# Depthwise filters as Toeplitz products per channel, and chunk products with the four heads on four tiles of the array

## What is computed

```python
def _L1_attn_ref(hidden_states, ...):                # H, DK, DV, CHUNK = 4, 32, 32, 32
    q, k, v_direct = conv(h @ Wq), conv(h @ Wk), conv(h @ Wv)     # 4 taps, silu
    beta = sigmoid(h @ Wb)
    delta_out = _delta_rule_chunkwise(q, k, v_direct, beta)
    paths = [_fir(v_direct, f) for f in (fir_w3, fir_w7, fir_w15, fir_w31)] + [delta_out]
    hmid = gelu(concat([h] + paths) @ router_W1 + router_b1)
    probs = softmax((hmid @ router_W2 + router_b2) / tau)
    ctx = sum(probs[..., i:i+1] * paths[i] for i in range(5))
    ...                                                # gate with v_direct, norm, Wo

def _fir(x, filt):            # causal depthwise filter: each channel has its own taps
    y[t, c] = sum over j < K of filt[c, j] * x[t - (K - 1) + j, c]     # K = 3, 7, 15, 31

def _delta_rule_chunkwise(q, k, v, beta, chunk=32):
    A = kb @ kc.T per chunk;  T = I + tril(A, -1);  inv = T^-1
    u = inv @ vc;  w = inv @ kbc
    for each of the 4 chunks:                          # S is the state, 32 x 32 per head
        u_adj = u_i - w_i @ S
        o = q_i @ S + tril(q_i @ k_i.T) @ u_adj
        S = S + k_i.T @ u_adj
```

## Time and profile before

| | |
|---|---|
| median of 3 runs | 1063.66 us |
| all three | 1063.66, 1056.33, 2446.21 us |
| span of the profiled execution | 1056.7 us |
| PE, DVE, ACT, POOL busy | 986.0, 735.5, 667.3, 331.7 us |
| instructions | 21902 |

### The profile page before, as it was taken

One profiled execution on the slowest core, in us unless ns is written; L12 is line 12 of the kernel. 1 busy time (PEld: TensorE's weight loads), 2 busy tenths in 40 slices (PEclk: granted clock), 3 DMA queues, 4 the chain that ended last, 5 costly groups with the idle time before them and its releaser, 6 DMA issues.

```text
span 1056.7 us, 21902 instructions
## 1 busy us (share of the span) xinstructions
PE 986.0 (93%) x7958; PEld 642.1 (61%) x7958; DVE 735.5 (70%) x2802; ACT 667.3 (63%) x1508; POOL 331.7 (31%) x720
## 2 busy tenths in 40 slices
PE   7989899999997989999999999999978999999996
PEld 4777475544446566568776756654436675677675
DVE  2656779788978766557544688887887786857523
ACT  4499998875532224676988777847533335677753
POOL 3775342524022011435332422241320022423321
PEclk9999999999986879999999999999986999999999
DMA  9300001031441110010000000204442010000001
GB/s 320 139 2 1 1 1 51 2 80 44 89 86 37 19 36 27 11 41 21 2 11 1 11 1 21 50 12 96 95 91 43 11 32 11 11 11 2 11 1 30
DMA packets 71930, 41.23 MB, mean 39 GB/s; under 512 B 52368, under 2 KB 64144, under 8 KB 71568
## 3 DMA queue, kind: packets, MB, share of 16 engines
q1 hardware_dynamic: 71824, 39.84, 14.6%
HBM read 30.92 MB, written 8.91 MB: 38 GB/s over the span
## 4 chain that ended last, share of the span: by engine, by line
PE 48%; DVE 27%; ACT 15%; POOL 4%; issue 3%; DMA 2%; SPq 1%; POOLq 0%; ACTq 0%; DVEq 0%
PE psum L1060 6%; DVE pool L1541 5%; DVE sol_t L1546 4%; PE psum L953 4%; ACT pool L1770 4%; PE psum L521 4%; DVE pool L1490 3%; PE psum L1050 3%; PE psum L883 3%; PE psum L796 2%; PE psum L794 2%; PE psum L822 2%; PE psum L1046 2%; PE psum L1044 2%; PE psum L922 2%
## 5 line engine op out<-in xcount | busy, mean ns | idle before, releaser
L1756 ACT ACTIVATE pool<-psum 128x512 f32<-128x512 f32 x144 | 84.2, 600 | 87.9 <-PE psum L883 38.9
L1770 ACT ACTIVATE pool<-pool,small 128x128 f32<-128x128 f32 x224 | 91.7, 487 | 37.6 <-POOL small L2135 37.5
L521 PE MATMUL psum<-sb_const,pool 128*128 128x128 f32 x672 | 100.0, 283 | 12.2 <-ACT pool L1770 8.1
L2130 POOL TENSOR_SCALAR small<-small 128x4 f32<-128x4 f32 x88 | 22.4, 254 | 272.2 <-DVE small L1132 270.7
L521 PEld LDWEIGHTS psum<-sb_const,pool 128*128 128x128 f32 x672 | 78.2, 144 | 47.7 <-issue 23.4
L883 PE MATMUL psum<-pool,firw 128*32 128x512 f32 (+7 forms) x960 | 105.4, 581 | 0.0
L2133 POOL TENSOR_TENSOR small<-small,minus_half 128x4 f32<-128x4 f32 x88 | 93.3, 1061 | 7.3
L953 PE MATMUL psum<-pool,sb_l1a 128*128 128x512 f32 x192 | 92.3, 634 | 0.7 <-ACT pool L1756 0.7
L1060 PEld LDWEIGHTS psum<-sb_l1f,pool 128*128 128x128 f32 x640 | 78.2, 192 | 14.5 <-issue 12.6
L1060 PE MATMUL psum<-sb_l1f,pool 128*128 128x128 f32 x640 | 83.3, 278 | 0.0
L1363 DVE TENSOR_TENSOR pool<-pool,psum 128x512 f32<-128x512 f32 x80 | 52.6, 680 | 31.3 <-ACT pool L1895 12.9
(11 more groups left out here) (427 smaller groups left out, 2248.2 us busy)
## 6 DMA issues: line engine op xcount, KB each, us to landing
pool<-scratch_kk SPq DMA_DIRECT2D x18, 256.0 KB, 3.7
pool<-in_cF SPq DMA_DIRECT2D x16, 256.0 KB, 3.5
pool<-in_xF SPq DMA_DIRECT2D x8, 256.0 KB, 6.0
pool<-in_x SPq DMA_DIRECT2D x8, 256.0 KB, 6.2
scratch_xt<-pool SPq DMA_DIRECT2D x8, 256.0 KB, 2.0
pool<-scratch_xt SPq DMA_DIRECT2D x8, 256.0 KB, 3.1
scratch_kk<-pool SPq DMA_DIRECT2D x32, 64.0 KB, 1.9
scratch_xt<-pool SPq DMA_DIRECT2D x16, 128.0 KB, 2.6
```

Of the source, the lines that this page charges most:

```text
L521: m = e.transpose(f.ap[:, part(b)], src[:, part(b)], ident)
L1756: e.activation(slot(g, i), f.ap, ACT.Copy).then_inc(f.emptied, 1)
L1770: m = e.activation(dst[:, part(b)], src[:, part(b)], ACT.Identity, bias=v["nm"][:, b:b + 1], scale=v["r"][:, b:b + 1])
```

## The change

**Filters.** v of the group (time-major, slot 2) goes to a padded DRAM array with 32 zero rows ahead of each entry. Four DMAs read it back in windows: partition i of quarter r holds row 16 n + i of the channels 32 r to 32 r + 31, for each block n of 16 time steps. Two more DMAs inside SBUF cut this into "this window" and "the window one block earlier". A table `toeplitz` [128, 32, 80] holds for every channel the taps of the four filters as 16-column Toeplitz blocks (64 columns), and another 16 columns for the part of the longest filter that reaches into the earlier window. b_fir.k now means channel quarter k, not filter length: for every channel one matmul of 32 rows, 32 weights (the windows of that channel, read at a stride of 32 elements) and 64 columns of the table, and one of 16 columns for the longest filter. The result has (block, channel) on the wrong axes for the rest of the kernel, so it goes to DRAM in pieces of 16 elements (b_fs) and is read back by channel (b_fl). b_r and b_mx wait for that.

**Chunk products.** b_u and b_p keep their 16 products a step, but head h now lies on rows and columns 32h to 32h + 31 (b_p: columns), so neighbours in the order use different tiles. For that the right side and the inverses are laid out by head: new DMA steps b_rs and b_rl (right side out and back), and b_xt apart from b_xo. b_p's subtraction is 128x128 instead of 32x512. b_u's copy is four pieces of 32x128: two by DVE, two by ACT, the second of which waits for DVE.

**The rest.** A set-up, lay_windows, builds the table with 97 DMAs in two rounds behind the weight loads. GpSimd zeroes the table at the start; b_ez is gone. Three constants that are used once move to a slot of group 0. ORDER is a new table (1839 entries instead of 1775).

```diff
+TB, NBLK, NROW = 16, P // 16, P // 16 + 2
+NVF = 5
...
-    firw, itau = sb("firw", [P, nfg * 4, CH]), sb("inverse_tau", [P, NH])
+    toeplitz, itau = sb("toeplitz", [P, CH, NVF * TB]), sb("inverse_tau", [P, NH])
+    lags = nc.dram_tensor("scratch_taps", (P, NVF * TB), F32, kind="Internal").ap()
+    padded = nc.dram_tensor("scratch_v", (NB, P + CH, P), F32, kind="Internal").ap()
+    paths = nc.dram_tensor("scratch_fir", (NG, 4, CH, P, TB), F32, kind="Internal").ap()
...
         def b_sh(g, k):
-            o.wait_ge(sem("v_made"), g + 1)
+            f = fill("b_vT", g)
+            o.wait_ge(f.emptied, f.n)
             upper_half(o, g)
-            e.dma_start(kept, slot(g, 5)).then_inc(sem(f"v_out{a}"), 16)
-            o.wait_ge(sem(f"v_out{a}"), 16 * (g // NA + 1))
-            for s in range(4):
-                e.dma_start(vsh[32 * s:32 * s + 32, :, s:],
-                            kept.rearrange("(c p) m -> p c m", c=4)[:, :, 0:GT - s]).then_inc(sem(f"shifted{a}"), 16)
+            e.dma_start(padded[g * GB:g * GB + GB, CH:, :].rearrange("b t c -> t b c"), b4(slot(g, 2))).then_inc(*path(g))
+            moved(o, g, "v")
+            for r in range(4):
+                src = bass.AP(padded.tensor, padded[g * GB].offset + CH * r, [[P, CH], [TB * P, GB * NROW - 1], [1, CH]])
+                e.dma_start(windows(g)[CH * r:CH * r + CH, 0:GB * NROW - 1], src).then_inc(*path(g))
+
+        def b_sw(g, k):
+            moved(o, g, "rows")
+            for early in range(2):
+                src = windows(g).rearrange("p (b n) c -> p b (n c)", b=GB)[:, :, CH * (1 - early):CH * (NBLK + 1 - early)]
+                e.dma_start(slot(g, 8 + 2 * early, 2).rearrange("p (b m) -> p b m", b=GB), src).then_inc(*path(g))
+
+        def b_fs(g, k):
+            f = fill("b_fir", g, "s", k)
+            o.wait_ge(f.emptied, f.n)
+            dst = paths[g, k].rearrange("n p t -> p n t")
+            e.dma_start(dst, slot(g, 3 + k).rearrange("p (n t) -> p n t", t=TB)).then_inc(*path(g))
+
+        def b_fl(g, k):
+            moved(o, g, "sums")
+            by_channel = paths[g].rearrange("r (u f) (j n) t -> j (r u) f (n t)", f=4, j=4)
+            for j in range(4):
+                e.dma_start(slot(g, 3, 4)[j:P:4].rearrange("p (f m) -> p f m", f=4), by_channel[j]).then_inc(*path(g))
...
         def b_fir(g, k):
-            vsh = slot(g, 8, 4).rearrange("p (c b t) -> p c b t", c=4, b=GB)
-            kgs = [kg for ff, kg in FIR_GROUPS if ff == k]
-            for n, kg in enumerate(kgs):
-                for c in range(4):
-                    col = FIR_GROUPS.index((k, kg)) * 4 + c
-                    m = e.matmul(b4(f.ap)[32 * c:32 * c + 32, :, 4 * kg:], firw[:, col, :],
-                                 vsh[:, c, :, 0:P - 4 * kg], start=n == 0, stop=n == len(kgs) - 1)
+            o.wait_ge(sem("toeplitz_laid"), 32 + 16 * 16 * len(FIRS) + 16 * (CH - 1))
+            moved(o, g, "windows")
+            shifted = [slot(g, 8 + 2 * early, 2).rearrange("p (n c) -> p n c", c=CH) for early in range(2)]
+            f, r_ = begin("b_fir", g, "s", k), slice(CH * k, CH * k + CH)
+            for u in range(8):
+                for early in (0, 1):
+                    for j in range(4):
+                        c, j_ = 4 * u + j, slice(32 * j, 32 * j + 32)
+                        lo, hi = (48, 64) if early else (0, 64)
+                        m = e.matmul(f.ap[j_, 64 * u + lo:64 * u + hi], shifted[early][r_, :, c],
+                                     toeplitz[r_, c, 64 * early:64 * early + hi - lo], start=not early, stop=bool(early))
             m.then_inc(f.filled, 1)
...
         def b_p(g, k):                                 # PE
-            for q in range(NP):
-                m = e.matmul(hd(f.ap)[CH * c:CH * c + CH, q, :], kkt[0:CH * c, q, CH * c:CH * c + CH],
-                             hd(slot(g, 14))[0:CH * c, q, :], start=True, stop=True)
+            for b in range(GB):
+                for h in range(NH):
+                    q = h * GB + b
+                    m = e.matmul(f.ap[CH * h:CH * h + CH, DH * b:DH * b + DH], kkt[0:CH * c, q, CH * c:CH * c + CH],
+                                 hd(slot(g, 14))[0:CH * c, q, :], start=True, stop=True)
...
         def b_u(g, k):                                 # PE
-            src = hd(slot(g, 12 if c else 14))
-            for q in range(NP):
-                m = e.matmul(hd(f.ap)[r_, q, :], hd(slot(g, 13))[r_, q, :], src[r_, q, :], start=True, stop=True)
+            for b in range(GB):
+                for h in range(NH):
+                    h_, n = slice(CH * h, CH * h + CH), b * 4 + c
+                    m = e.matmul(f.ap[h_, DH * b:DH * b + DH], hd(slot(g, 13))[h_, n, :], hd(slot(g, 12))[h_, c * GB + b, :],
+                                 start=True, stop=True)
...
         def b_r(g, k):
-            got("b_fir", g, "s", 3)
+            moved(o, g, "paths")
...
         def b_p(g, k):                                 # DVE
-            e.tensor_tensor(slot(g, 12)[r_], slot(g, 14)[r_], f.ap[r_], ALU.subtract).then_inc(f.emptied, 1)
+            f, rest = full("b_p", g, "s", k), slot(g, 12)[:, P * (k + 1):P * (k + 2)]
+            e.tensor_tensor(rest, rest, f.ap[:, 0:P], ALU.subtract).then_inc(f.emptied, 1)
+
+        def b_u(g, k):                                 # DVE
+            f, r_ = full("b_u", g, "s", k), slice(CH * k, CH * k + CH)
+            for h in range(NH // 2, NH):
+                m = e.tensor_copy(slot(g, 14)[r_, part(h)], f.ap[CH * h:CH * h + CH, 0:P])
+            m.then_inc(sem("u_halves"), 1)
...
         def b_u(g, k):                                 # ACT
-            e.activation(slot(g, 14)[r_], f.ap[r_], ACT.Copy).then_inc(f.emptied, 1)
+            e.activation(slot(g, 14)[r_, part(0)], f.ap[0:CH, 0:P], ACT.Copy)
+            o.wait_ge(sem("u_halves"), n_half["b_u", k, g])
+            e.activation(slot(g, 14)[r_, part(1)], f.ap[CH:2 * CH, 0:P], ACT.Copy).then_inc(f.emptied, 1)
```

More of the change, by code:

```diff
@@ L1 @@
+import itertools
 from contextlib import ExitStack
@@ L313, in wt @@
         n = width - lo if n is None else n
+        if piece in once_used:
+            return spare[piece][:, lo:lo + n]
+        first -= sum(cols[p_][apart][1] for apart, of in once_used.items() if of == p_ and cols[p_][apart][0] < first)
         return tiles[p_][:, first + lo:first + lo + n]
@@ L363, in landed, with windows, path, moved @@
         for p_ in parts:
-            own.wait_ge(sem("ld_" + p_), 16)
+            own.wait_ge(sem("ld_" + p_), 16 * landing.get(p_, 1))
+    def windows(g):
+        return slot(g, 3, 3)[:, 0:GB * NROW * CH].rearrange("p (n c) -> p n c", c=CH)
+    MOVED = {"v": 1, "rows": 5, "windows": 7, "sums": 11, "paths": 15}
+    def path(g):
+        return sem(f"path{g % NA}"), 16
+    def moved(own, g, what):
+        own.wait_ge(sem(f"path{g % NA}"), 16 * (g // NA * MOVED["paths"] + MOVED[what]))
+    CHUNKED = {"diagonals": 4, "triangles": 6, "inverses": 8, "turned": 12}
+    def chunks(g):
+        return sem(f"chunks{g % NA}"), 16
+    def chunked(own, g, what):
+        own.wait_ge(sem(f"chunks{g % NA}"), 16 * (g // NA * CHUNKED["turned"] + CHUNKED[what]))
     MADE = {"s_a": 1, "s_m": 2, "s_f": 3, "s_b1": 4, "s_b2": 5, "s_g1": 6}
```

298 lines of the change are left out of this document (172 added, 126 removed).

## The result

The changed kernel takes 1067.49 us (median of 7 runs, 1064.89 to 1070.72), the kernel before 1060.6 in the same comparison. The ratio is 1.0064, with a 95% interval of 1.0038 to 1.0091: 0.6% slower, clear of the scatter, but no change by the bound of 2%. The forecast was 993, 6.6% faster. The measured time lies 2.5 us inside the range, which ended at 1070, but on the slow side of the kernel before: the width of the range took it in, not the reasoning.

A forecast was written before the change was run, and what follows sets the result against it. PE sets the pace, DVE next in the filter and chunk stretches. Of 111 us off PE (filters 59, chunk products 52) 75 count, transfers add 4: 1063.7 - 75 + 4 = 993 us, range 940 to 1070.

The forecast's parts named there:

- its 75 for 111: Whole kernel: of 111 us taken off PE, 75 reach the time, the middle between 38 and all 111.
- The price of a filter round: Filters on PE: 0.058 us for a 64-column round of four matmuls, 0.032 for a 16-column one.
- I take 46: Filters on PE: 46 us for all 4096 instructions, 59 less than before, between bounds of 37 and 106.
- rival (b): Filter and chunk starts don't get cheaper: filters stay at 106 us, half the chunk gain goes; 1050 us, chance 0.20.
- rival (c): Clock falls with filter matmuls on 32 of 128 rows: clock loss doubles, 1033 us, chance 0.10.
- The bound by DVE: In the two filter and chunk stretches DVE is next after PE: if nothing else moved, 400 us shrinks by only 38.
- The chunk products on PE: b_u and b_p, heads on four tiles: 0.43 us a step instead of 1.35, 52 us less on PE.
- The new walk: New instruction order: may spread DVE's work so that all 111 us count; no cost of its own was priced.
- The transfers: DMA and its queue: longer round trips and more DMAs on SP, mostly hidden by the walk; +4 us.
- rival (d): The filter sums' 64-byte stores block SP's queue and delay transfers others wait for: 1118 us, chance 0.12.
- The cover of 25 entries: Group 3, last b_fs to b_r: 25 walk entries, 14 us, hide the sums' trip of 8 to 16 us.
- The signs named in advance: Wrong if a filter step takes 3 us, mean clock is under 0.93, or PE idle grows from 71 to over 160.

The follow-up runs named there:

- e1: Changed kernel with each filter product's 32 weights read from neighbouring values instead of 128 bytes apart (wrong values filtered); ratio 0.9984 to the kernel before.
- e5: Changed kernel with contiguous weight reads and four row groups in turn for neighbouring filter products (wrong values, wrong order); ratio 0.9978 to the kernel before.
- e2: Changed kernel with each filter product contracting over all 128 rows instead of 32 (sums not the filters'); ratio 0.9907 to the kernel before.
- e8: Changed kernel with half as many filter products, twice the columns each, all on 128 rows (sums not the filters'); 1012.96 us, ratio 0.9534 to the kernel before.
- e6: Changed kernel with half as many filter products, each with twice the columns, still on 32 rows (sums not the filters'); ratio 0.9599 to the kernel before.
- h3: New walk alone: filters and chunk products of the kernel before, in the new order; 1078.7 us, ratio 1.0158 to the kernel before.
- h1: New walk and new chunk products, with the filters of the kernel before; 1050.1 us, ratio 0.9886 to the kernel before.
- g1: New walk, new chunk products, old filters, with b_u evacuated by four ACT copies instead of two ACT and two DVE; 1044.6 us, ratio 0.9864 to the kernel before.
- g2: Kernel before in its own walk with the new chunk products, b_u evacuated by four ACT copies; 1045.67 us, ratio 0.9872 to the kernel before.
- e7: Changed kernel with filter sums stored as 128 pieces of 2 KB a transfer instead of 4096 of 64 bytes (DRAM order differs); ratio 1.0051 to the kernel before.
- e9: Changed kernel without the filter sums' stores and loads through DRAM (later lines read misplaced values); ratio 1.0061 to the kernel before.
- e3: Changed kernel with neighbouring filter products on four different groups of 32 rows instead of the same one (wrong channel order); ratio 0.9952 to the kernel before.

## Why the prediction was wrong

In the prediction's units (us of time; its 75 for 111 applied to each half) it read: filters -40, chunk products -35, walk nothing, transfers +4. The runs show +19, -29, +17 and 0. The differences (59 + 6 + 17 - 4 = 78), less the 3 us by which the kernel before has come out faster than the 1063.7 of the sum, are the 75 us between 993 and 1067. (The 7.0 us between that median and the span were mostly scatter: the changed kernel's profiled run is 1.8 us longer than its span.)

- *The price of a filter round* failed, and with it the sum. "I take 46" lay near the lower of its two bounds, 37 and 106, argued from L643's eight instructions. They are too few to reach a break in the supply: the price of a short stream was carried over to one of 512. Busy and breaks together are 108 us, beyond the upper bound, so the 59 us that PE was to lose are nothing. This was rival (b), given 0.20, and of its two reasons both exist: the spread reads cost 20 us on the line (e1), but the supply takes them back. Its own time, 1050, fell 17 us short; the clock and the walk were not in it. The floor of 25 ns that it cites from the Trainium skill, page "TensorE: Matmul & The Clock Gate", section "Back-to-back issue gap", does not hold here: the filters' 23 ns lie near it, but they fall to 17 in e5, and 32 instructions in 0.45 us, L1040, are 14.
- *The clock* was rival (c), added as if it shut out (b). The missing part of the clock went from 0.041 to 0.104, more than the doubling that it reckoned at 40 us. All rows give 17 us back in e2, where the half-clock time goes from 221 to 113 us, though PE's other lines had lost 21 to 32 us of work to it. Both rivals held at once, and the text gave that no chance. With the number of instructions and the clock both mended (e8, 56 us under the changed kernel) the filter half is worth 19 - 56 = -37, close to the -40 of the prediction, though e8 does not compute the filters. So the mechanism, that time follows what PE is freed of, held, and the price was wrong. That -37 meets -40 is in part luck: e8's filters still take 57.5 us on PE, not 46.
- *The bound by DVE* in the two stretches was wrong as a share for both halves. For e6 all of PE's freed time reached the end; for the chunk products 29 of 54 did, since PE's idle time rose by 25 (h3 to h1).
- *The chunk products on PE* were right: 54 us in h3 to h1, 52 forecast, and 0.45 for 0.43 a step. What was missing is a look at who is queued behind what: "short ACT copy beside two DVE copies, then a second ACT copy, about the old 0.59" priced the copies and not DVE's row before them.
- *The new walk* was taken as neutral or helpful. By itself it cost 17 (h3), and what it gives is room for DVE's copies: with them the chunk products lose 21 us in the old walk and win 29 in the new one, and without them the two walks are equal (g1, g2).
- *The transfers*: the trip of the sums cost nothing, so rival (d) is excluded for this walk by e7 and e9. The cover of 25 entries held, and PE never waited for the Toeplitz table. PE did wait 5.0 us for the windows, which no run takes away, so the 0 above is for the sums' trip alone.
- *The signs named in advance*: a mean clock under 0.93 came true; a step of 128 instructions took 3.03 to 3.08 us in group 4, where the steps stand apart, over the 3 that were to tell (b), and in group 3, shown above, 128 of them took 2.8 us and 4.1 from break to break. PE's idle time grew to 109, not over 160, and 109 is about what the forecast itself held (a span of 986 less 880 busy). PE's work is 954 for 880: the whole shortfall lies in work that did not go, not in new waits beyond those allowed for.

## What to carry to other kernels

Price a dense stream of small matmuls by its number of instructions over some hundreds of them, breaks included: a row of eight or thirty-two tells the start, not the supply. If a rewrite multiplies narrow products, look for the form with half the instructions even at the same columns, and with more rows to each. Before an evacuation is split between two engines, look at what stands ahead of it on each: the later of the two rows sets the step.

## What the runs showed of the hardware

- PE's program came in packets of 16 KB, 256 entries, in one group of the changed kernel 2.3 to 2.6 us before PE went on; a long stream of filter products stood still there 0.4 to 1.7 us at every 128th matmul. Faster starts did not shorten the 8.28 us that two packets took (e1).
- With PE busy all the time (5.00 of 5.00 us), the granted clock fell to 0.50 with filter products on 32 rows and stayed at 1.00 with 128 rows (e2). Over the whole kernel the mean was 0.896 and 0.946.
- Weight loads with 128 bytes from column to column made line 998 20 us longer than contiguous ones (e1: 94.6 and 74.7, 4096 instructions). Four products in a row on the same 32 rows instead of four groups of rows cost 18.5 (e3: 94.6 and 76.1).
